# Table of expert places in a routed mixture of experts: 192, 152 and 128 rows, in place of 192, 160 and 128

## The reference

```python
logits = jnp.einsum('th,eh->te', x, gate_w)
probs = jax.nn.softmax(logits, axis=-1)
topk_w, topk_idx = jax.lax.top_k(probs, TOP_K)          # TOP_K = 8, 64 experts
combine = (jax.nn.one_hot(topk_idx, NUM_EXPERTS, dtype=x.dtype) * topk_w[..., None]).sum(axis=1)
def step(acc, inp):
    w13_e, w2_e, c = inp
    g = x @ w13_e[:INTER].T
    u = x @ w13_e[INTER:].T
    h = jax.nn.silu(g) * u
    o = h @ w2_e.T
    return (acc + c[:, None] * o, None)
```

## Time and profile before

| | |
|---|---|
| median of 3 runs | 569.99 us (566.71 to 570.38) |
| the profiled execution | 565.74 us, span 563.9 us |
| mean granted TensorE clock | 0.858 of full speed |
| busy in the span | PE 73%, DVE 61%, ACT 33%, POOL 26% |
| moved by DMA | 82.96 MB, 147 GB/s over the span |

### The profile page before, as it was taken

The page is one execution under the profiler, slowest core; times in us unless marked ns, Lnnn a source line. Parts: engine busy times, 40 slices in busy tenths (PEclk is TensorE's granted clock), DMA queues, the critical chain, the costliest instruction groups (busy, mean ns, idle before and its releaser), DMA issues.

```text
span 563.9 us, 9233 instructions
## 1 busy us (share of the span) xinstructions
PE 410.0 (73%) x2738; PEld 345.4 (61%) x2738; DVE 344.6 (61%) x1053; ACT 184.4 (33%) x377; POOL 148.1 (26%) x156
## 2 busy tenths in 40 slices
PE   5344652400899999999621778799889998998796
PEld 3233442400798888998420555698578867896695
DVE  4987876289344444444236585488867976790664
ACT  3122210200233333343360134523544264417321
POOL 4017675756000000000177813430434000000000
PEclk9966565655799999999855679899999999999999
DMA  7999222236699999999333202110212000000000
GB/s 240 427 410 393 91 99 76 93 123 259 185 286 319 318 314 314 339 391 394 128 98 99 81 16 57 42 53 3 58 29 76 10 1 0 19 2 2 2 20 19
DMA packets 36789, 82.96 MB, mean 147 GB/s; under 512 B 6032, under 2 KB 16144, under 8 KB 34960
## 3 DMA queue, kind: packets, MB, share of 16 engines
q1 hardware_dynamic: 22896, 55.83, 28.4%
q0 software_dynamic: 6144, 16.79, 9.2%
q10 hardware_dynamic: 7712, 9.90, 4.9%
HBM read 50.44 MB, written 31.92 MB: 146 GB/s over the span
## 4 chain that ended last, share of the span: by engine, by line
PE 52%; issue 12%; DVE 9%; DMA 8%; POOL 7%; ACT 6%; SPq 4%; another core or an unknown queue 1%; DVEq 0%; POOLq 0%; ACTq 0%
PE PS L584 11%; PE PS L594 7%; POOL slots_in L439 7%; DMA slots_in<-GB 5%; PE PS L673 5%; PE PS L647 4%; PE PS L571 3%; PE PS L750 3%; PE PS L686 3%; PE PS L688 2%; PE PS L687 2%; PE PS L768 2%; PE PS L778 2%; PE PS L735 2%; SPq L334 1%
## 5 line engine op out<-in xcount | busy, mean ns | idle before, releaser
L451 POOL DMA_INDIRECT GB<-slots_out,IDXG x64 | 69.4, 1084 | 226.9 <-SPq L367 140.5
L584 PE MATMUL PS<-XTE,WR 128*128 128x128 f32 (+2 forms) x512 | 79.5, 299 | 0.0
L439 POOL DMA_INDIRECT slots_in<-XNA,IDX x64 | 65.1, 1017 | 38.7 <-issue 19.7
L584 PEld LDWEIGHTS PS<-XTE,WR 128*128 128x128 f32 x512 | 70.4, 193 | 0.3 <-ACT XTE L896 0.2
L1278 DVE TENSOR_TENSOR HE<-SGE,PS 128x128 f32<-128x128 f32 (+2 forms) x64 | 20.0, 312 | 69.0 <-ACT SGE L905 66.8
L594 PE MATMUL PS<-WR,HE 128*80 128x256 f32 (+2 forms) x198 | 53.4, 380 | 0.3 <-DVE HE L1278 0.3
L896 ACT COPY XTE<-PS 128x256 f32<-128x256 f32 (+2 forms) x64 | 26.3, 411 | 73.3 <-PE PS L571 72.2
L686 PE MATMUL PS<-XH,WGH 128*128 128x256 f32 x160 | 50.0, 312 | 0.0
L571 PE MATMUL PS<-CF,XE 80*128 80x80 f32 (+2 forms) x198 | 28.4, 257 | 26.2 <-DMA XE<-slots_in 26.2
L673 PE MATMUL PS<-WD,XW 128*128 128x256 f32 x160 | 41.6, 383 | 5.8 <-DVE TH L1356 5.8
L688 PE MATMUL PS<-XH,WGL 128*128 128x256 f32 x160 | 45.4, 284 | 0.0
(11 more groups left out here) (226 smaller groups left out, 811.8 us busy)
## 6 DMA issues: line engine op xcount, KB each, us to landing
WR<-in_wexp SPq DMA_DIRECT2D x64, 384.0 KB
slots_in<-GB SPq DMA_DIRECT2D x12, 1024.0 KB, 18.6
XE<-slots_in SPq DMA_DIRECT2D x24, 160.0 KB, 4.3
slots_out<-OE ACTq DMA_DIRECT2D x24, 160.0 KB, 4.2
XE<-slots_in SPq DMA_DIRECT2D x29, 128.0 KB, 4.4
slots_out<-OE ACTq DMA_DIRECT2D x29, 128.0 KB, 4.8
WGU<-in_wgu SPq DMA_DIRECT2D x1, 2560.0 KB
XE<-slots_in SPq DMA_DIRECT2D x11, 192.0 KB, 3.9
```

What stands on the lines that cost most here:

```text
L439: pool.indirect_dma_start(out=xs, out_offset=bass.IndirectOffsetOnAxis(ap=IDX[:, t, j:j + 1], axis=0), in_=XNA[:, t, :], in_offset=None, b ...
L451: pool.indirect_dma_start(out=GB[:, t % BT, j, :], out_offset=None, in_=ys, in_offset=bass.IndirectOffsetOnAxis(ap=IDXG[:, t, j:j + 1], ax ...
L584: last = mm(psGE[place % 2][:, a, 0:cap(place)], W13[:, k, a, :], XTE[:, place % 2, k, 0:cap(place)], start=(k == 0), stop=(k == KC - 1))
```

## The change

The number of slots at places 8 to 10 goes from 192 to 152, and at places 11 to 34 from 160 to 152. Places 0 to 7 keep 192 and places 35 to 63 keep 128. In all 9352 slots are computed, in place of 9664. A place of 152 slots is laid out on 76 partitions of 2048 bytes.

```diff
@@ -34,7 +34,7 @@
 CAP = 192
 
 
-CLASSES = ((0, 192), (11, 160), (35, 128))
+CLASSES = ((0, 192), (8, 152), (35, 128))
 SP_ = CAP // 2
 SLOTS = E0 * CAP
 SLOTS_OUT = sum([size for first, size in CLASSES if e >= first][-1] for e in range(E0))
```

## The result

The changed kernel takes 611.71 us (607.2 to 614.41, 4 runs) against 570.04 (566.71 to 570.38, 4 runs) of the kernel before: the ratio is 1.0741, 95% interval 1.0688 to 1.0794. It is slower by 42 us, with 3.2% fewer slots. The profiled execution took 607.20 us, with a span of 605.4 against 563.9.

What follows compares the result with a forecast made beforehand. Four DMA engines were to bound the expert stage, 4.16 us a place against PE's 2.21. The sum's 45 us plus 3 for the clock, +48 on 569.99, gave 618 us, range 601 to 650.

Steps and rivals of the forecast that it cites:

- The number of engines: Loads and stores of 152 slots: 76 rows go to 4 of 16 DMA engines, always the same, 19 rows apiece.
- The rate of one engine: Expert stage: each of the four DMA engines moves 24.6 GB/s, so a place costs 4.16 us.
- rival 2's fast side: Four engines in the expert stage at 26.7 GB/s each: 151 us for 4.03 MB, 602 us; no separate chance given.
- Rival 2's slow side: Four engines in the expert stage at 19.8 GB/s each: 204 us for 4.03 MB, 654 us; chance 0.10.
- rivals 1 and 3: Slot transfers: rows over all 16 engines, 567.6 us, chance 0.09; or one engine, about 880 us, 0.03 together with rival 4.
- rival 4: An expert has more tokens than its place and `all_tokens` runs: +670 us; chance 0.03 together with one engine per odd transfer.
- The +45 us of the sum: Expert stage: four engines carry 4.03 MB in 164 us, so the last XE lands at about 316 us, 45 later.
- the sum by places: Expert stage: about 20 places x (4.16 - 2.27) = 38 us, after PE's lead of some 6 places is used up.
- the end of the lead and the last class: Rest of the 45 us beyond 38: PE's lead running out, and the 128-slot places, 1.67 us each beside SP's 1.76.
- The 3 us for the clock: PE, about half busy in each 4.16 us, loses clock; returning to full at the last class costs 3 us, between 0 and 6.
- The gain on PE: Expert stage: PE saves about 2.4 us at places 8 to 34, no gain while PE waits.

Runs made afterwards that it cites:

- 84 and 75 rows together: Kernel before with 168 slots at places 0 to 7, 150 at 8 to 29, 128 from 30: 563.67 us against 570.2, ratio 0.9881.
- the run in which PE's part stands alone: Kernel before, places 8 to 34 load and store 160 slots, but PE, ACT and DVE compute 152: 566.61 us, ratio 0.9971.
- narrow loads: Kernel before with 160 slots computed and stored at places 8 to 34, but only 152 loaded (76 rows): 585.04 us, ratio 1.031.
- narrow stores alone: Changed kernel with loads of places 8 to 34 widened to 160 slots, stores left at 76 rows: 580.59 us, ratio 1.0218 against the kernel before.

## Why the prediction was right, point by point

**The number of engines** was the step on which everything hung, and no row of before showed a transfer of 76 rows. It was inferred from the closing packets of other row counts. The counts of ACT's queue with 74, 75, 76, 77, 79 and 84 rows came out as 7124, 7502, 7232, 7448, 7232 and, with 84 and 75 rows together, 7660, each as the largest divisor up to 16 has it. That they are always the same engines is shown too, though no view names an engine. With loads and stores of several places asked for at once, other engines for each would lift the slices between the weights over four engines' worth, and with 79 rows over one's; they show 98 to 105 and 25 to 26 GB/s. The Trainium skill, page "DMA: Bandwidth & Descriptors", section "Why a DMA increments its semaphore by 16 and not by 1", states both; by that rule the runs here agree for all six row counts.

**The rate of one engine**, taken as 24.6 GB/s, is confirmed within some 7%. The slices between the weights show 24.5 to 26. With the bytes that the most loaded engine carries from the first refill to the last slots, worked out as in the prediction, the stages are:

| rows | engines | MB of the fullest engine | stage, us |
|---|---|---|---|
| 76 | 4 | 4.03 | 170.9 |
| 74 | 2 | 6.03 | 247.3 |
| 79 | 1 | 10.67 | 432.9 |

Between the first two 76.4 us go with 2.00 MB, 26.2 GB/s; between the last two 185.6 with 4.64, 25.0. The rate lies between the forecast's and the 26.7 GB/s of rival 2's fast side (602 us), as the time does. Rival 2's slow side, with 19.8 GB/s and 654 us, has fallen, and rivals 1 and 3, all 16 engines and a single one, with it. The flag's rival 4 didn't come about: the stage has its 64 places and layer 1 follows.

**The +45 us of the sum** became 42.8, in nearly the shares that the prediction gave. The flip of place 35 began at 227.20 before and at 262.87 now, 35.7 us later, where the sum by places had 38. From there to the last flip it took 50.4 us, against 43.7 before: 6.7 more, where the prediction left 7 for the end of the lead and the last class. That is 1.80 us a place, near SP's pace of 1.76. One piece of the chain at the seam of the two classes is easily misread:

```profile
267.94 0.91 PE PS L584 x8
...
268.88 9.04 DMA slots_out<-OE
...
278.69 0.70 PE PS L594 x2
```

It isn't a pause of 9 us. The piece goes from the issue of a store to its landing, and PE works meanwhile, as the stage view shows:

```profile
260.00:280.00 20.00, 18.50 (x119) 15.46 (x118) 6.50 (x18) 5.74 (x19) 0.00 (x0) 0.91 0.83 277
```

DVE's copies and PE's flips of the last class in the view by form (busy us, mean ns, idle us and what ended them):

```profile
L1271 DVE COPY OE<-PS 128x256 f32<-128x256 f32 x29 | 12.2, 422 | 8.3 <-DMA slots_out<-OE 7.9 <-PE PS L594 0.5
L571 PE MATMUL PS<-CF,XE 128*128 128x128 f32 x58 | 12.0, 290 | 2.3 <-DMA XE<-slots_in 2.1
```

The last narrow stores are still under way when the cheap places begin, and DVE waits 7.9 us in all for buffers of `OE` (1.7 before). Hardly any of that reaches PE, whose waits for XE in this class are 2.1 us (0.5 before). That is part of the 6.7 us; no row names the rest.

**The 3 us for the clock** are the term for which the runs give no support. The prediction had PE busy for about half of each place, beside a row with a granted clock of 0.54. PE was busy for 41.84 of 60 us, and the granted clock fell from 1.00 only to 0.86. The multiplications of L594 took 434 ns on average in place of 379, and in front of the flips of the narrow places PE still waited 27.8 us. By form, the first line from the kernel before:

```profile
L594 PE MATMUL PS<-WR,HE 128*80 128x256 f32 x96 | 24.6, 379 | 0.0
```

```profile
L594 PE MATMUL PS<-WR,HE 128*76 128x256 f32 x108 | 32.9, 434 | 0.0
L571 PE MATMUL PS<-CF,XE 76*128 76x76 f32 x108 | 13.2, 247 | 27.8 <-DMA XE<-slots_in 27.8
```

So the slower instructions filled a wait that was there anyway. That they cost nothing is argued from this; no run holds the clock and changes the rest. With the term the forecast is 618, without it 615, and 611.71 was measured.

**The gain on PE**, 2.4 us, is near what the stage gives up in the run in which PE's part stands alone, 2.6 us in one execution each. In the time of the whole it isn't clear of no change.

## What to carry to other kernels

A DMA's cost depends on how its rows divide among the engines, so a size chosen by the work (how many slots are needed) has to be checked for its divisors: here 150 and 154 were free, 152 cost 42 us and 158 over 300. Where a mean DMA share is low and an engine waits for DMA all the same, count the packets: those beyond the rows tell how many engines carry each transfer. Then look at the slices between the large transfers, where the few engines stand alone. And cheaper instructions on the busiest engine gain nothing if the same edit makes a second resource, here four of sixteen engines, the slower one.

## What the hardware showed that I had not expected

The issue of a DMA can block its queue. SP's 64 issues of XE, with the shortest, median and longest time in ns, in the changed kernel, in the one of 74 rows and in the one of 79:

```profile
L350 SPq DMA_DIRECT2D XE<-slots_in x64: 294/332/3315, 139.9 to 306.1; - x64
```

```profile
L350 SPq DMA_DIRECT2D XE<-slots_in x64: 277/333/5838, 135.6 to 380.3; - x64
```

```profile
L350 SPq DMA_DIRECT2D XE<-slots_in x64: 269/333/7832, 136.0 to 566.1; - x64
```

In the kernel before the longest is 348 ns. So with few engines full, an issue waits up to 3.3, 5.8 and 7.8 us. The issues of WR, which would use the idle engines too, take up to 3.6, 6.3 and 12.6 us in these three kernels, against 0.9 before. With 74 and 79 rows ACT's issues of stores do it as well, up to 3.0 and 11.9 us. That this adds little to the time is argued from the runs with narrow loads and narrow stores alone, and from the four engines that never ran dry; how many transfers a queue takes before it blocks was not tried.
